# Two-batch attention heads on one core: rotary products of batch 1 in swapped buffers, and new orders for TensorE, ScalarE, VectorE and the sync queue

## What is computed

```python
x = layernorm(hidden)                                   # (2, 512, 512)
q     = (x @ Wq.T).reshape(B, S, H, K)                  # 16 heads of 128
q_big = einsum('bshk,hkq->bshq', q, w_kc_q)             # 384 wide
q_big = q_big * cos + rotate_half(q_big) * sin
kv_r  = rope(ctx)                                       # (2, 1024, 128)
q_r   = einsum('bshq,hqr->bhsr', q_big, W_qr)           # 64 wide
k_r   = einsum('bld,hdr->bhlr', kv_r, W_kr)
attn  = softmax(einsum('bhsr,bhlr->bhsl', q_r, k_r))
ctx_c = einsum('bhsl,bld->bhsd', attn, kv_r)
out   = hidden + (ctx_c with w_kc_kv and Wo, summed over heads)
```

## Time and profile before

| what | value |
|---|---|
| time, median of 3 runs | 862.25 us (861.66 to 864.22) |
| the profiled execution | 863.58 us, of which the span from first to last instruction is 861.4 us |
| busy share of the span | TensorE 87%, VectorE 89%, ScalarE 67%, GpSimd 67% |
| mean granted TensorE clock | 0.974 |
| a head of the loop, VectorE's low 7 to the next | about 42.2 us where odd, 41.1 us where even |

### The profile page before, as it was taken

The page is one execution under the profiler, slowest core; times in us unless marked ns, Lnnn a source line. Parts: engine busy times, 40 slices in busy tenths (PEclk is TensorE's granted clock), DMA queues, the critical chain, the costliest instruction groups (busy, mean ns, idle before and its releaser), DMA issues.

```text
span 861.4 us, 12568 instructions
## 1 busy us (share of the span) xinstructions
PE 749.9 (87%) x3258; PEld 484.7 (56%) x3268; DVE 763.8 (89%) x1026; ACT 573.7 (67%) x838; POOL 576.7 (67%) x581
## 2 busy tenths in 40 slices
PE   3678998989999999999999989999998675868996
PEld 3555565756666666666566656665665432424543
DVE  5899899989998999899989998999999756598896
ACT  2587677767766867687667766776776586584342
POOL 5759674867486757766776668576848464867562
PEclk9999999999999999999999999999999797899999
DMA  9226866676768576847676766767569989500000
GB/s 329 81 55 116 171 128 151 122 164 134 152 116 169 115 164 132 170 111 168 119 157 138 148 129 137 149 137 151 125 146 233 258 193 227 210 0 25 13 24 37
DMA packets 294405, 118.50 MB, mean 138 GB/s; under 512 B 271856, under 2 KB 278000, under 8 KB 294128
## 3 DMA queue, kind: packets, MB, share of 16 engines
q1 hardware_dynamic: 293568, 116.68, 61.1%
q10 hardware_dynamic: 816, 1.57, 0.5%
HBM read 49.02 MB, written 2.10 MB: 59 GB/s over the span
## 4 chain that ended last, share of the span: by engine, by line
PE 30%; POOL 25%; DVE 14%; issue 12%; DMA 8%; SPq 5%; ACT 4%; POOLq 1%; DVEq 0%; ACTq 0%
PE banks L1419 18%; POOL rot_cos L1055 6%; PE scores L1720 4%; DMA load<-in_pack 4%; POOL rot_lo L1063 4%; SPq L943 4%; PE scores L1507 3%; POOL rot_hi L1061 3%; DVE neg_max L1323 2%; DVE rows L1330 2%; PE banks L1735 2%; POOL rot_sin L1046 2%; DMA pt<-rows 2%; POOL wq_lo L388 2%; POOL wo_lo L388 2%
## 5 line engine op out<-in xcount | busy, mean ns | idle before, releaser
L1185 ACT ACTIVATE scores<-scores,neg_max 128x1024 f32<-128x1024 f32 x128 | 139.2, 1087 | 54.3 <-DVE neg_max L1323 52.7
L1419 PE MATMUL banks<-pt,v_hi 128*128 128x512 f16 x512 | 156.2, 387 | 15.2 <-DMA pt<-rows 15.2
L1330 DVE SCALAR_TENSOR_TENSOR rows<-scores,rows 128x1024 f16<-128x1024 f32 x128 | 154.8, 1219 | 9.7 <-ACT rows L1196 8.5
L1323 DVE TENSOR_REDUCE neg_max<-scores 128x1 f32<-128x1024 f32 x128 | 155.5, 1216 | 3.4 <-PE scores L1507 3.1
L1055 POOL TENSOR_TENSOR rot_cos<-rot_cos,rot_sin 128x512 f32<-128x512 f32 x93 | 119.1, 1281 | 45.5 <-DVE rot_sin L1297 41.3
L1196 ACT ACTIVATE rows<-scores 128x1024 f16<-128x1024 f32 x128 | 130.9, 1022 | 5.2
L1063 POOL TENSOR_TENSOR rot_lo<-rot_cos,rot_hi 128x512 fp32r<-128x512 f32 x93 | 119.5, 1285 | 7.8
L1159 ACT CAST cv_hi<-banks 128x512 fp32r<-128x512 f32 x64 | 37.5, 586 | 104.9 <-PE banks L1419 103.8
L1419 PE MATMUL banks<-pt,v_lo 128*128 128x512 f16 x256 | 98.5, 385 | 0.0
L1318 DVE SCALAR_TENSOR_TENSOR acc<-banks,inv,acc 128x512 f32<-128x512 f32 x128 | 91.2, 744 | 3.9
L1419 PEld LDWEIGHTS banks<-pt,v_hi 128*128 128x128 f16 x512 | 44.8, 99 | 83.0 <-issue 42.3
(11 more groups left out here) (211 smaller groups left out, 1813.3 us busy)
## 6 DMA issues: line engine op xcount, KB each, us to landing
load<-in_pack SPq DMA_DIRECT2D x15, 320.0 KB, 3.5
raw_chunk<-in_out_w SPq DMA_DIRECT2D x8, 512.0 KB, 4.2
raw_chunk<-in_gate_w SPq DMA_DIRECT2D x8, 512.0 KB, 4.5
raw_chunk<-in_val_w SPq DMA_DIRECT2D x8, 512.0 KB, 4.7
raw<-in_gate_w SPq DMA_DIRECT2D x8, 512.0 KB, 5.2
raw<-in_val_w SPq DMA_DIRECT2D x8, 512.0 KB, 5.6
raw<-in_out_w SPq DMA_DIRECT2D x8, 512.0 KB, 6.9
load<-in_pack SPq DMA_DIRECT2D x15, 256.0 KB, 3.3
```

The lines of the kernel that those rows point to most:

```text
L1185: nc.scalar.activation(scores[:, u % 2, :], scores[:, u % 2, :], ACT.Exp, bias=neg_max[:, u:u + 1], accum_out=sums[:, u:u + 1]).then_inc(e ...
L1323: nc.vector.tensor_reduce(neg_max[:, u:u + 1], scores[:, u % 2, :], AX, ALU.max, negate=True).then_inc(max_ready, 1)
L1330: nc.vector.scalar_tensor_tensor(out=rows[:, u % ROWS, 1, :], in0=scores[:, u % 2, :], scalar=WEIGHT_LIFT, in1=rows[:, u % ROWS, 0, :], op ...
L1419: mm = nc.tensor.matmul(out, ws[a], xs[c], start=first and n == 0, stop=last and n == 2)
```

## The change

Three things are changed. First, VectorE writes two products of batch 1 elsewhere: of B 1 0 the cosine product goes to `rot_sin` chunk 0 (its sine product goes to `rot_sin` chunk 1 as before), and of B 1 1 the sine product goes to `rot_cos` chunk 0. The sums are the same. B 1 0 then writes nothing into `rot_cos`, so it needs no part of C 0 ahead of it, and it is put behind part 0 in place of part 1. Second, the orders of even and odd heads change on TensorE, ScalarE and VectorE; head 0 has the same changes near its end (B 1 0; exp 5 ahead of high 4; O 0 1 ahead of max 7). Third, the loads and turns on the sync queue are put in another order. The numbers of the lots get names in GpSimd's orders and in that of head 14, which changes nothing there. The diff, cut:

```diff
 EVEN_PE = (
-    ("K", 1, 0), ("score", 0), part(0, 4, A0), part(1, 4, A0), part(2, 4, A0), ("K", 1, 1), part(3, 4, A0),
+    ("K", 1, 0), ("score", 0), part(0, 4, A0), part(1, 4, A0), ("K", 1, 1), part(2, 4, A0), part(3, 4, A0),
...
-    part(4, 8, V1), part(5, 8, V1), ("score", 2), part(6, 8, V1), part(7, 8, V1),
+    part(4, 8, V1), ("score", 2), part(5, 8, V1), part(6, 8, V1), part(7, 8, V1),
-    ("O", 1, 2, "last"), ("O", 1, 3, "last"), part(0, 4, A1),
+    ("O", 1, 2, "last"), part(0, 4, A1), ("O", 1, 3, "last"),
-    ("M",), part(0, 3, C0), part(1, 3, C0), ("B", 1, 0, "next"), part(2, 3, C0), ("B", 1, 1, "next"), ("score", 5),
+    ("M",), part(0, 3, C0), ("B", 1, 0, "next"), part(1, 3, C0), part(2, 3, C0), ("B", 1, 1, "next"), ("score", 5),
 ODD_PE = (
-    ("B", 0, 2, "next"), part(0, 8, V1), part(1, 8, V1), part(2, 8, V1), part(3, 8, V1), ("score", 2), part(4, 8, V1),
+    ("B", 0, 2, "next"), ("score", 2), part(0, 8, V1), part(1, 8, V1), part(2, 8, V1), part(3, 8, V1), part(4, 8, V1),
-    ("M",), part(0, 3, C0), part(1, 3, C0), ("B", 1, 0, "next"), part(2, 3, C0),
+    ("M",), part(0, 3, C0), ("B", 1, 0, "next"), part(1, 3, C0), part(2, 3, C0),
-    ("K", 0, 0, "next"), part(4, 8, V0), ("K", 0, 1, "next"), part(5, 8, V0), ("B", 1, 2, "next"), part(6, 8, V0),
+    ("K", 0, 0, "next"), ("K", 0, 1, "next"), part(4, 8, V0), ("B", 1, 2, "next"), part(5, 8, V0), part(6, 8, V0),
 EVEN_ACT = (
-    ("exp", 0), ("high", 0), ("exp", 1), ("high", 1), ("B", 0, 2, "next"), V1,
-    ("exp", 2), ("high", 2), ("exp", 3), ("double", 1, "last"), ("high", 3), A1, ("abs", 2),
-    ("M",), ("exp", 4), ("high", 4), C0, ("exp", 5), ("high", 5), ("B", 1, 2, "next"), ("double", 0, "next"), V0,
+    ("exp", 0), ("high", 0), ("B", 0, 2, "next"), ("exp", 1), ("high", 1), V1,
+    ("exp", 2), ("high", 2), ("double", 1, "last"), ("exp", 3), ("high", 3), A1,
+    ("M",), ("exp", 4), ("abs", 2), C0, ("exp", 5), ("high", 4), ("high", 5), ("B", 1, 2, "next"), V0, ("double", 0, "next"),
 ODD_ACT = (
-    ("exp", 1), ("high", 1), ("B", 0, 2, "next"), V1,
+    ("exp", 1), ("B", 0, 2, "next"), ("high", 1), V1,
-    ("high", 3), ("double", 1, "last"), A1, ("M",), ("abs", 0), ("exp", 4), C0, ("high", 4),
+    ("high", 3), ("abs", 0), ("double", 1, "last"), A1, ("M",), ("exp", 4), C0, ("high", 4),
-    V0, ("double", 0, "next"), ("exp", 6), ("high", 6), ("abs", 1), ("exp", 7), C1,
+    ("double", 0, "next"), V0, ("exp", 6), ("high", 6), ("exp", 7), ("abs", 1), C1,
 EVEN_DVE = (
-    ("O", 1, 0, "last"), ("O", 1, 1, "last"), ("low", 2), ("O", 1, 2, "last"), ("O", 1, 3, "last"), ("low", 3), A1,
+    ("O", 1, 0, "last"), ("low", 2), ("O", 1, 1, "last"), ("low", 3), ("O", 1, 2, "last"), ("O", 1, 3, "last"), A1,
-    ("max", 6), ("O", 0, 0), ("max", 7), ("low", 6), ("O", 0, 1), ("O", 0, 2), ("O", 0, 3), C1,
+    ("max", 6), ("O", 0, 0), ("O", 0, 1), ("max", 7), ("low", 6), ("O", 0, 2), ("O", 0, 3), C1,
 ODD_DVE = (
-    ("O", 1, 0, "last"), ("low", 2), ("O", 1, 1, "last"), ("O", 1, 2, "last"), ("low", 3), ("O", 1, 3, "last"), A1,
+    ("O", 1, 0, "last"), ("low", 2), ("O", 1, 1, "last"), ("low", 3), ("O", 1, 2, "last"), ("O", 1, 3, "last"), A1,
-    ("max", 6), ("O", 0, 0), ("max", 7), ("O", 0, 1), ("low", 6), ("O", 0, 2), ("O", 0, 3), C1,
+    ("max", 6), ("max", 7), ("O", 0, 0), ("O", 0, 1), ("low", 6), ("O", 0, 2), ("O", 0, 3), C1,
 EVEN_SP = (
-    ("turn", 7, "last"), ("lot", 2), ("lot", 3), ("chunk", 0), ("turn", 0), ("turn", 1), ("turn", 2), ("turn", 3),
-    ("turn", 4), ("turn", 5), ("lot", 0), ("turn", 6), ("lot", 1),
+    ("turn", 7, "last"), ("lot", WRK), ("turn", 0), ("lot", WVO), ("chunk", 0), ("turn", 1), ("turn", 2), ("turn", 3),
+    ("lot", WQ), ("turn", 4), ("turn", 5), ("lot", WC), ("turn", 6),
 ODD_SP = (
-    ("turn", 7, "last"), ("lot", 2), ("pair",), ("turn", 0), ("lot", 3), ("chunk", 0), ("turn", 1), ("turn", 2),
-    ("turn", 3), ("turn", 4), ("chunk", 1), ("lot", 0), ("turn", 5), ("lot", 1), ("turn", 6),
+    ("turn", 7, "last"), ("lot", WRK), ("chunk", 0), ("pair",), ("turn", 0), ("turn", 1), ("turn", 2), ("lot", WVO),
+    ("turn", 3), ("lot", WQ), ("turn", 4), ("chunk", 1), ("turn", 5), ("lot", WC), ("turn", 6),
...
-                    nc.vector.tensor_tensor(rot_cos[:, c, :], src, t["cos"][:, c, :], ALU.mult)
+                    cos_to, sin_to = (rot_sin if b and c == 0 else rot_cos), (rot_cos if b and c == 1 else rot_sin)
+                    nc.vector.tensor_tensor(cos_to[:, c, :], src, t["cos"][:, c, :], ALU.mult)
                     if c < 2:
-                        return nc.vector.tensor_tensor(rot_sin[:, 1 - c, :], src, t["sin"][:, c, :], ALU.mult)
+                        return nc.vector.tensor_tensor(sin_to[:, 1 - c, :], src, t["sin"][:, c, :], ALU.mult)
```

More of the change, by code:

```diff
@@ L101 @@
 EVEN_ACT = (
-    ("high", 7, "last"), ("K", 1, 0), A0, ("K", 1, 1), ("exp", 0), ("high", 0), ("exp", 1), ("high", 1),
-    ("B", 0, 2, "next"), V1, ("exp", 2), ("high", 2), ("exp", 3), ("double", 1, "last"), ("high", 3), A1, ("abs", 2),
-    ("M",), ("exp", 4), ("high", 4), C0, ("exp", 5), ("high", 5), ("B", 1, 2, "next"), ("double", 0, "next"), V0,
-    ("exp", 6), ("high", 6), ("exp", 7), C1,
+    ("high", 7, "last"), ("K", 1, 0), A0, ("K", 1, 1), ("exp", 0), ("high", 0), ("B", 0, 2, "next"), ("exp", 1),
+    ("high", 1), V1, ("exp", 2), ("high", 2), ("double", 1, "last"), ("exp", 3), ("high", 3), A1, ("M",), ("exp", 4),
+    ("abs", 2), C0, ("exp", 5), ("high", 4), ("high", 5), ("B", 1, 2, "next"), V0, ("double", 0, "next"), ("exp", 6),
+    ("high", 6), ("exp", 7), C1,
 )
 ODD_ACT = (
[L108 to L111, removed]
+    ("high", 7, "last"), A0, ("exp", 0), ("high", 0), ("exp", 1), ("B", 0, 2, "next"), ("high", 1), V1, ("exp", 2),
+    ("high", 2), ("exp", 3), ("high", 3), ("abs", 0), ("double", 1, "last"), A1, ("M",), ("exp", 4), C0, ("high", 4),
+    ("exp", 5), ("high", 5), ("K", 0, 0, "next"), ("K", 0, 1, "next"), ("B", 1, 2, "next"), ("double", 0, "next"), V0,
+    ("exp", 6), ("high", 6), ("exp", 7), ("abs", 1), C1,
 )
@@ L114 @@
     ("low", 7, "last"), ("K", 1, 0), A0, ("max", 0), ("K", 1, 1), ("max", 1), ("low", 0), ("B", 0, 0, "next"),
[L115 to L116 removed]
+    ("B", 0, 1, "next"), ("low", 1), ("max", 2), ("B", 0, 2, "next"), V1, ("max", 3), ("O", 1, 0, "last"), ("low", 2),
+    ("O", 1, 1, "last"), ("low", 3), ("O", 1, 2, "last"), ("O", 1, 3, "last"), A1, ("max", 4), ("M",),
     ("B", 1, 0, "next"), ("B", 1, 1, "next"), ("max", 5), C0, ("low", 4), ("low", 5), ("B", 1, 2, "next"), V0,
[L118 removed]
+    ("max", 6), ("O", 0, 0), ("O", 0, 1), ("max", 7), ("low", 6), ("O", 0, 2), ("O", 0, 3), C1,
 )
@@ L121 @@
     ("low", 7, "last"), ("max", 0), A0, ("max", 1), ("low", 0), ("B", 0, 0, "next"), ("B", 0, 1, "next"), ("low", 1),
[L122 to L126, removed]
+    ("B", 0, 2, "next"), ("max", 2), V1, ("max", 3), ("O", 1, 0, "last"), ("low", 2), ("O", 1, 1, "last"), ("low", 3),
+    ("O", 1, 2, "last"), ("O", 1, 3, "last"), A1, ("max", 4), ("M",), ("B", 1, 0, "next"), ("B", 1, 1, "next"),
+    ("max", 5), C0, ("low", 4), ("low", 5), ("K", 0, 0, "next"), ("K", 0, 1, "next"), ("B", 1, 2, "next"), V0,
+    ("max", 6), ("max", 7), ("O", 0, 0), ("O", 0, 1), ("low", 6), ("O", 0, 2), ("O", 0, 3), C1,
 )
@@ L134 @@
     ("score", 2), ("M",), ("B", 0, 2, "next"), ("score", 3), ("K", 1, 0), A1, ("score", 4), part(0, 3, C0),
-    part(1, 3, C0), ("B", 1, 0, "next"), part(2, 3, C0), ("B", 1, 1, "next"), ("score", 5), part(0, 8, V0),
+    ("B", 1, 0, "next"), part(1, 3, C0), part(2, 3, C0), ("B", 1, 1, "next"), ("score", 5), part(0, 8, V0),
     part(1, 8, V0), part(2, 8, V0), part(3, 8, V0), part(4, 8, V0), ("B", 1, 2, "next"), part(5, 8, V0),
@@ L189 @@
 LATE_SP = (
-    ("turn", 7, "last"), ("lot", 2), ("turn", 0), ("lot", 3), ("chunk", 0), ("turn", 1), ("turn", 2), ("raw", 0, 0),
-    ("turn", 3), ("raw", 0, 1), ("raw", 1, 0), ("raw", 1, 1), ("raw", 2, 0), ("turn", 4), ("raw", 2, 1),
-    ("raw", 3, 0), ("turn", 5), ("raw", 3, 1), ("turn", 6),
+    ("turn", 7, "last"), ("lot", WRK), ("turn", 0), ("lot", WVO), ("chunk", 0), ("turn", 1), ("turn", 2),
+    ("raw", 0, 0), ("turn", 3), ("raw", 0, 1), ("raw", 1, 0), ("raw", 1, 1), ("raw", 2, 0), ("turn", 4),
+    ("raw", 2, 1), ("raw", 3, 0), ("turn", 5), ("raw", 3, 1), ("turn", 6),
 )
```

29 lines of the change are left out of this document (14 added, 15 removed).

## The result

The changed kernel takes 873.79 us, median of 3 runs (871.81 to 875.84), where the kernel before took 862.25 us: a ratio of 1.0123, 95% interval 1.0097 to 1.0149. The forecast was 863.9 us and its range ended at 869.0. The profiled execution took 871.81 us with a span of 869.7 us, 8.3 us more than the 861.4 us before. Cut at VectorE's low 7 of head 1 and at the end of head 14, the loop is 9.1 us longer (594.45 for 585.36 us), the opening 0.1 and the tail 0.7 us shorter.

What follows compares the result with a forecast made beforehand. VectorE was taken as the bound, so the loop could be shortened only by its idle time. Score 2's 2.3 us less B 1 0's 0.7 gave +1.6 us on the 862.25 median, 863.9 us, range 860.5 to 869.0.

Steps and rivals of the forecast that it cites:

- the sync queue's odd orders: Odd heads' loads: chunk 0 ahead of key pair, WVO behind turn 2; GpSimd later but covered, 0, bounds 0 to 1 us a head.
- the sum: Whole kernel: 2.3 us for score 2 less 0.7 for B 1 0, +1.6 us; everything else counted as nothing.
- rot 1 0 behind WVO: Sign that the prediction is wrong: GpSimd comes late to rot 1 0 because it stands behind WVO; no size given.
- Turn 7: Odd heads: the later turn would let V 1 start at 6.74 us, hidden by score 2 at 6.99, 0.25 us to spare.
- sentence on ring order: Sync queue: each DMA engine takes descriptors in ring order, so a turn behind a load ends later; no separate size.
- score 2 ahead of V 1: TensorE, odd heads: score 2 waits for low 0 and delays V 1, 0.33 us a head, 2.3 us in all, bounds 0.4 to 3.3.
- high end: Upper bound of score 2's wait in an odd head, 0.47 us, with 0.12 us for TensorE starting from a standstill.
- Even heads: High 4 behind exp 5: VectorE waits 0.92 us at low 4, hidden behind GpSimd, cost nothing; 6.4 us if cover failed.
- B 1 0 and the buffers: All 14 loop heads: B 1 0 one part earlier gains 0.05 us each, 0.7 us, bounds 0 to 1.4; swapped buffers cost nothing.
- the late turn: Rival, odd heads: turn 7 lands 1 us later, V 1 starts 0.75 us later, 5.3 us, 869.2 us in all; chance 0.24.
- The faster case: Rival, even heads: waits at V 0, low 6 and C 1 go, 7.1 us won, 856.8 us; chance 0.12.
- nothing: Rival, odd heads: the 0.33 us is taken up at VectorE's C 1 wait, about 862 us; chance 0.14.

Runs made afterwards that it cites:

- the swap: Changed kernel with the key pair ahead of chunk 0 again in the odd heads' sync queue: 867.98 us beside 864.23, ratio 1.0039.
- the two kernels where the turn alone holds V 1: Kernel before with WC ahead of turn 6 in even heads: 870.35 us; changed kernel with score 2 back behind V 1's part 3: 874.21 us.
- the runs with the old queue: Changed kernel with both sync-queue orders of the kernel before: 870.36 us; the same with WQ ahead of turn 4 in even heads: 865.42 us.

## Why the prediction was wrong

**The step that failed** is the one on the sync queue's odd orders: "Both make GpSimd later; it is covered by its own idle time", taken as 0 and bounded by 1 us a head. The idle time it names lies ahead of the sine product of B 1 2 and ahead of WVO, and both come after rot 0 2. But rot 0 2 has a customer before either: part 2 of C 0, with B 1 1 behind it on TensorE. The cover there was 2.07 us, and the pair's delay was 3.2. I asked how long GpSimd waits, and not who waits first for what it makes late. The delay itself was not worked out at all. By the swap, 2.4 of the 3.2 us hang on the chunk ahead of the pair (23.44 to 21.04 us); the 0.8 us that stay (21.04 for 20.21) go with WRK, which comes later behind the late turns, and the prediction had the late turns as a matter of V 1 alone. In the trace of the changed kernel the wait at B 1 1 adds up to 8.0 us over the odd heads, where the sum had 0; the wait at V 1 grew by 2.4 us, where the sum had 2.3. The swap that took the pair's part out won about 7 us (0.84%). The prediction's own sign for a late GpSimd was rot 1 0 behind WVO, one batch too late in GpSimd's order.

**Turn 7.** Forecast: V 1 by the turn at 6.74 us, hidden by score 2 at 6.99. Measured: 6.98 and 7.18 us in the two kernels where the turn alone holds V 1, and 7.08 behind score 2. That score 2 hides the turn was right, and the cover held with next to nothing to spare. What I missed is what the turn costs where score 2 has not moved: 1.2 us in head 7. The prediction's sentence on ring order had the turn end later behind a load on the ring; what the trace shows is a later issue, 2.59 us after the start of head 7 for 1.31, with 4.35 us from issue to landing for 4.28.

**score 2 ahead of V 1**: forecast 0.33 us a head, 0.35 in head 7; found 0.42 us in head 7's wait at V 1, and 0.4 us in the head once the pair is in time. Right in mechanism and near in size; the first two matmuls of score 2 start 0.34 us apart and the next 0.23, so 0.11 of the 0.12 us that the prediction kept for its high end was there. No run takes this term out by itself: wherever score 2 was put back, the late turn or WC's late split held the odd heads instead.

**Even heads**: forecast unchanged with a wait of 0.92 us at low 4, found 41.1 us with 0.84; from the end of B 1 1 to C 1 it is 431.04 - 417.28 = 13.76 us for 13.72. Right for the even head. As the runs with the old queue are read, high 4's move has a cost all the same, through turn 4 and WQ into the next odd head, and the new place of WQ takes it away again. The prediction saw neither, so that the two cancel in the changed kernel was luck.

**B 1 0 and the buffers**: forecast -0.7 us, not to be told from nothing. **Rivals**: the late turn came nearest, since it too is a queue order that costs time in odd heads, but its 869.2 us rested on V 1, whose wait grew by 0.42 us in head 7. The faster case and "nothing" had no part.

## What to carry to other kernels

When a step is made late, follow what it makes to its first customer, in the order of the customer's own queue; the idle time of the late engine counts only ahead of that customer. On a queue shared by small loads that are wanted soon and large ones that are not, let the small ones go first: here the swap of two neighbours was worth 7 us. Two costly edits can cover each other, as score 2 and the late turn did here, and an edit that looks free can cost once its neighbours change, so a part is judged in the company it will run in.
